# Four graph layers on one core: gathers written out with their indices read from the column table, and the last layer's plain one-hot rows compared on GpSimd

## The reference, cut to what matters

```python
x = x + L0(h)        # three rounds of normalised neighbour sums
msg = h[row] * norm[:, None]; out = segment_sum(msg, col)          # L1, then relu
x = x + L2(h)        # mean over neighbours, two 64x64 products
x = concatenate([nodes[senders], nodes[receivers], edges], axis=-1)      # L3
h = relu(x @ msg_W1 + msg_b1)
messages = relu(h @ msg_W2 + msg_b2)
agg = segment_sum(messages, receivers, num_segments=3125)
y = relu(concatenate([nodes, agg]) @ node_W1 + node_b1) @ node_W2 + node_b2
return nodes + layernorm(y)
```

## Time and profile before

| | |
|---|---|
| median of 3 runs | 1106.03 us (1105.96 to 1106.82) |
| span of the profiled execution | 1325.8 us |
| mean granted TensorE clock | 0.862 |
| POOL busy | 592.2 us (45%), of it 503.5 us in the 514 gathers |
| DVE busy | 830.9 us (63%) |
| ACT busy | 452.6 us (34%) |
| PE busy | 1006.6 us (76%) |

### The profile page before, as it was taken

The page is one execution under the profiler, slowest core; times in us unless marked ns, Lnnn a source line. Parts: engine busy times, 40 slices in busy tenths (PEclk is TensorE's granted clock), DMA queues, the critical chain, the costliest instruction groups (busy, mean ns, idle before and its releaser), DMA issues.

```text
span 1325.8 us, 24512 instructions
## 1 busy us (share of the span) xinstructions
PE 1006.6 (76%) x6145; PEld 618.1 (47%) x6145; DVE 830.9 (63%) x2605; ACT 452.6 (34%) x1035; POOL 592.2 (45%) x763
## 2 busy tenths in 40 slices
PE   3788887996667767667696787777787878777685
PEld 2566553553444545445355444434444534444443
DVE  8988877357645556757657554565555555555556
ACT  3677771011434333334013232232232323222232
POOL 6533330000665666654003656555555555555550
PEclk9677778998887788877797899999888998999997
DMA  2000006001111111100523533333333333333331
GB/s 54 2 0 0 0 0 243 1 1 22 24 23 19 20 21 22 21 19 17 168 63 75 138 81 79 76 76 76 77 73 77 75 71 77 75 73 78 72 75 34
DMA packets 145110, 72.80 MB, mean 55 GB/s; under 512 B 111917, under 2 KB 136698, under 8 KB 144922
## 3 DMA queue, kind: packets, MB, share of 16 engines
q1 hardware_dynamic: 127224, 54.98, 16.0%
q0 software_dynamic: 16448, 16.88, 6.9%
q10 hardware_dynamic: 1378, 0.22, 0.1%
HBM read 59.66 MB, written 12.35 MB: 54 GB/s over the span
## 4 chain that ended last, share of the span: by engine, by line
PE 41%; another core or an unknown queue 20%; issue 16%; DVE 12%; ACT 6%; DVEq 2%; POOL 1%; ACTq 1%; DMA 1%; SPq 1%; POOLq 0%
PE seg L1628 10%; PE big L1658 5%; PE big L1552 4%; PE seg L1683 4%; PE seg L1755 3%; PE big L1791 3%; PE seg L1802 2%; ACT A L1345 2%; PE seg L1566 2%; PE big L1781 1%; ACT A L1466 1%; PE seg L1696 1%; ACT A L1472 1%; PE seg L1823 1%
## 5 line engine op out<-in xcount | busy, mean ns | idle before, releaser
L1221 POOL DMA_INDIRECT A<-table,idx x338 | 327.3, 968 | 260.6 <-ACT idx L1317 154.2
L1221 POOL DMA_INDIRECT pair<-table,idx x176 | 176.2, 1001 | 126.8 <-ACT idx L1317 65.0
L1755 PE MATMUL seg<-A 128*128 128x384 f16 (+1 forms) x624 | 137.6, 370 | 44.5 <-issue 19.1
L1466 ACT COPY A<-big 128x512 f32<-128x512 f32 x104 | 61.1, 587 | 249.7 <-remote 156.7
L1345 ACT CAST A<-big 128x500 f32 x208 | 125.4, 603 | 48.0 <-PE big L1557 25.9
L1791 PE MATMUL big<-A 128*128 128x512 f32 x208 | 114.1, 631 | 33.6 <-ACT A L1466 28.3
L2033 DVE COPY A<-seg 128x512 f32<-128x512 f32 x52 | 36.0, 691 | 162.3 <-remote 150.6
L1683 PE MATMUL seg<-A,cur 128*64 128x160 f32 x750 | 94.8, 353 | 46.0 <-issue 45.9
L1397 ACT COPY A<-big 128x500 f32<-128x500 f32 x120 | 66.5, 576 | 181.4 <-remote 113.8
L1755 PEld LDWEIGHTS seg<-A 128*128 128x128 f16 x624 | 60.3, 106 | 140.5 <-issue 91.0
L1658 PE MATMUL big<-A 128*128 128x300 bf16 x480 | 106.1, 367 | 18.8 <-issue 10.4
(11 more groups left out here) (307 smaller groups left out, 1809.6 us busy)
## 6 DMA issues: line engine op xcount, KB each, us to landing
A<-in_edge_attr_dram SPq DMA_DIRECT2D x103, 128.0 KB
A<-drel_flat SPq DMA_DIRECT2D x104, 126.0 KB
spilled_adjacency<-A SPq DMA_DIRECT2D x1, 7074.0 KB, 21.8
A<-spilled_adjacency SPq DMA_DIRECT2D x6, 1152.0 KB, 11.8
A<-table,idx POOLq DMA_INDIRECT x338
A<-pr_table SPq DMA_DIRECT2D x104, 31.5 KB
pair<-table,idx POOLq DMA_INDIRECT x176
A<-low_flat SPq DMA_DIRECT2D x78, 32.0 KB
```

The source lines that it names most:

```text
L1221: pool.indirect_dma_start(out=row(q, j), out_offset=None, in_=table, in_offset=bass.IndirectOffsetOnAxis(ap=idx[:, q, j:j + 1], axis=0)).t ...
L1466: nc.scalar.copy(x_t[:, r, :], big[:, r, :]).then_inc(x_t_ready[r], 1)
L1755: op = nc.tensor.matmul(made[:, 0:held.shape[2] * D], hot_low[:, u, m, :], held[:, k, :, :], start=(m == 0 and k == 0), stop=(m == 3 and k ...
```

## The change: what it does

1. POOL's two gather loops are written out: 176 and 338 gathers stand one after the other in its stream, and each reads its index column straight from `src_i`. The tile `idx`, its semaphores and ACT's 148 copies are gone. In layer 1 a gather waits for `seg_done[q]` alone, in the last layer for `transposed` alone.
2. The last layer's plain one-hot rows are made on POOL, one instruction of 128 x 42 for each tile (416 in all), one behind each gather slot, six groups behind the gathers (HOTS_LAG). The first of a group waits for `seg_done` of its pair of groups. DVE's 52 instructions of 128 x 336 are gone.
3. PE's `window_sums` waits for the one-hot rows of both groups.

```diff
-            def gathers(g, row, slot_free):
-                pool.wait_ge(table_stored, 32 * (g + 1))
-                with pool.Fori(0, (IT1, IT)[g]) as it:
-                    for q in range(Q):
-                        pool.wait_ge(idx_ready[q], g * IT1 + it + 1)
-                        slot_free(it, q)
...
+            def gather_tile(row, tile, landed):
+                pool.indirect_dma_start(
+                    out=row, out_offset=None, in_=table,
+                    in_offset=bass.IndirectOffsetOnAxis(ap=src_i[:, tile:tile + 1], axis=0)).then_inc(landed, 16)
+            def gathers1():
+                pool.wait_ge(table_stored, 32)
+                pool.wait_ge(ev("src_kept"), 1)
+                for it in range(IT1):
                     for q in range(Q):
+                        pool.wait_ge(seg_done[q], 1 + it)
                         for j in range(G):
+                            gather_tile(row1(q, j), it * (Q * G) + q * G + j, gathered[q])
+            def gathers3():
+                pool.wait_ge(table_stored, 64)
+                for q in range(Q):
+                    pool.wait_ge(seg_done[q], 1 + IT1)
+                for g in range(GROUPS + HOTS_LAG):
+                    it, q = g // Q, g % Q
+                    if g < GROUPS:
+                        pool.wait_ge(transposed[q % 2], 1 + 2 * it + q // 2)
+                    for j in range(G):
+                        if g < GROUPS and not (q in MADE and j == 2):
+                            gather_tile(X[:, q, j, 0:D], it * (Q * G) + q * G + j, gathered[q])
+                        if g >= HOTS_LAG:
+                            tile_hots(g - HOTS_LAG, j)
+            def tile_hots(g, j):
+                it, q = g // Q, g % Q
+                if j == 0:
+                    pool.wait_ge(seg_done[q | 1], it + (1 + IT1))
+                op = pool.tensor_scalar(onehot3[:, q, j, :], iota_r[:, 0:GW], drel[:, g * G + j:g * G + j + 1], None, ALU.is_equal)
+                if j == G - 1:
+                    op.then_inc(onehot_ready[q], 1)
...
-            steps(act, [(0, next_idx), (2, node_relu), (3, copy_rows), (4, hidden), (5, message_relu)])
+            steps(act, [(2, node_relu), (3, copy_rows), (4, hidden), (5, message_relu)])
...
                 pe.wait_ge(msg_ready[1], k + 2)
+                pe.wait_ge(onehot_ready[q - 1], it + (IT1 + 1))
                 pe.wait_ge(onehot_ready[q], it + (IT1 + 1))
...
-            steps(dve, [(1, receivers), (5, message), (0, senders), (4, plain_hots), (0, node_norm),
+            steps(dve, [(1, receivers), (5, message), (0, senders), (0, node_norm),
```

More of the change, by code:

```diff
@@ L60 @@
 NODES_LAG = 5
+HOTS_LAG = 6
 OUTS = (slice(0, T // (G * Q) - NODES_LAG), slice(T // (G * Q) - NODES_LAG, NC))
@@ L834, in dense_path @@
         rdeg = sb("rdeg", [P, NC])
-        idx = sb("idx", [P, Q, G], I32)
         dst_c = pair[:, 0:TK]
@@ L981, in dense_path @@
         gathered = [sem(f"gathered{q}") for q in range(Q)]
-        idx_ready = [sem(f"idx_ready{q}") for q in range(Q)]
         onehot_ready = [sem(f"onehot_ready{q}") for q in range(Q)]
@@ L998, in dense_path @@
         table_ready, table_stored = sem("table_ready"), sem("table_stored")
-        gathers_begun = sem("gathers_begun")
         tail_loaded = sem("tail_loaded")
@@ L1214, in gathers @@
                     for q in range(Q):
-                        pool.wait_ge(idx_ready[q], g * IT1 + it + 1)
-                        slot_free(it, q)
-                        pool.sem_inc(gathers_begun, 1)
+                        pool.wait_ge(seg_done[q], 1 + it)
                         for j in range(G):
[L1219 to L1229, removed]
+                            gather_tile(row1(q, j), it * (Q * G) + q * G + j, gathered[q])
[12 more added lines that the diff above has]
+                            tile_hots(g - HOTS_LAG, j)
@@ L1276, in on_gpsimd @@
             pool.memset(acc_mem[D:2 * D, 0:NPAD], 0.0).then_inc(ev("lower_cleared"), 1)
-            gathers(0, row1, rows_summed)
+            gathers1()
             def clear_sums(k):
@@ L1290, in on_gpsimd @@
                 clear_sums(k)
-            gathers(1, lambda q, j: X[:, q, j, 0:D], rows_transposed)
+            gathers3()
         def steps(eng, stages, between=lambda s: None):
@@ L1314, in nodes_done @@
             return q == at and not (isinstance(it, int) and it < NODES_LAG)
-        def copy_idx(it, q):
-            nc.scalar.copy(idx[:, q, :], src_i[:, bass.ds(it * (Q * G) + q * G, G)]).then_inc(idx_ready[q], 1)
         def on_scalar(act):
@@ L1377, in on_scalar @@
                 copy_sums(n)
-            act.wait_ge(ev("src_kept"), 1)
-            for q in range(Q):
-                copy_idx(0, q)
             for k in range(ROUNDS):
@@ L1386, in on_scalar @@
                 nc.scalar.copy(acc_t[:, 4 * k * P:4 * k * P + n], seg[0:D, k % 2, 0:n]).then_inc(ev("conv1_t"), 1)
-            def next_idx1(it, q):
-                act.wait_ge(seg_done[q], 1 + it)
-                copy_idx(it, q)
             def keep_block(b, buf, more):
@@ L1409, in rows_behind @@
             def rows_behind(b, q):
-                summed = SUM_AT.get(b * Q + q - 1)
-                if summed is not None and summed + Q < Q * IT1:
-                    next_idx1(summed // Q + 1, summed % Q)
                 to_sum = SUM_AT.get(b * Q + q + 1)
@@ L1418, in on_scalar @@
                 keep_block(b, b % 2, rows_behind)
-            for q in range(Q):
-                act.wait_ge(seg_done[q], 1 + IT1)
-                copy_idx(0, q)
             copy_sums(3)
@@ L1454, in on_scalar @@
             act.wait_ge(ld_l3, 13 * 16)
[L1456 to L1460, removed]
             def copy_rows(it, q):
@@ L1879, in plain_hots1 @@
                                   drel[:, t:t + G].rearrange("p (j a) -> p j a", a=1).broadcast_to([P, G, GW]),
[L1880 to L1888, removed]
                                   ALU.is_equal).then_inc(onehot_ready[q], 1)
```

## The result

The changed kernel takes 1257.41 us (median of 4 runs, 1257.2 to 1262.54), the kernel before beside it 1106.42 (4 runs). The ratio is 1.137, 95% interval 1.135 to 1.139: 151 us slower. The forecast was 1164 us, 58 us slower, with a range of 1085 to 1225 us; the time lies above the range.

What follows compares the result with a forecast made beforehand. POOL, at 1.25 us a gather, was taken to bound both gather stages. Comparisons on POOL 62, less 4 for index copies and 0 for DVE's relief, gave +58 us on 1106: 1164 us, range 1085 to 1225.

Steps and rivals of the forecast that it cites:

- What bounds the kernel: Both gather stages: POOL at 1.25 us a gather bounds, about 447 us for the last layer, PE right behind.
- Index copies: ACT's 148 copies and POOL's waits for them go, both gather stages: 0 to 20 us gained, 4 taken.
- DVE's comparisons: Last layer: 25.8 us leave DVE, worth 0 to 10 us, taken as 0 while POOL bounds.
- The new waits: POOL's wait for `seg_done` and PE's second wait in `window_sums`: some tenths of a us or 0, latency hidden.
- POOL's comparisons: Last layer: 416 instructions of 128 x 42 on POOL, 0 to 0.60 us each, taken as 0.15, 62 us.
- Rival C: VectorE and GpSimd shut each other out in the last layer, 0.35 us a comparison: 1248 us; chance 0.10.
- Rival A: POOL's comparison fits into the 0.30 us pause behind each gather, only small gains remain: 1098 us; chance 0.27.
- Rival B: POOL's timed gather is shorter than in the profile, say 1.05 us, so POOL has slack: 1089 us; chance 0.16.

Runs made afterwards that it cites:

- undisturbed profile: Profile of the kernel before with POOL's two gather loops written out and ACT's index copies kept: 1106.61 us, ratio 0.9999, span 1107.2 us.
- written-out gathers: Kernel before with gathers written out, reading index columns directly, ACT's copies gone, comparisons left on DVE: 1103.33 us, ratio 0.9968; repeated 1102.53 us, ratio 0.9967.

## Why the prediction was wrong, point by point

*What bounds the kernel: right.* The stalls in the profile of before were taken for that execution's own and POOL's floor for real. The undisturbed profile of the same kernel has L3 at 428 us, where the step had 422 of gathers, and PE right behind it. A reading that had spent the profile's slack would have come out at no change. That the two floors are some 10 us apart is measured by the run with one gather less.

*Index copies: right in size.* 4 us were taken, 3.3 to 4.4 us measured (1106.61 less 1103.33 beside it, and 1106.88 of before less 1102.53 in the later pair). What became late next is `transposed`, as said. The place is off: the gain was to lie in layer 1, where POOL's waits for ACT turn out to be 0.6 us in the undisturbed profile, and of what was gained 1.3 to 2.6 us lie in the last layer. So there is some luck in the 4.

*DVE's comparisons: right.* 0 taken, 0 measured (1102.27 against 1102.53).

*The new waits: small, as said.* They were taken as 0; together with 416 fills they cost 7 us.

*POOL's comparisons: this step failed.* It took 0.15 us net each, 62 us. The measured price is (581.6 - 427.0) / 416 = 0.37 us, 155 us (L3 of the change from 649.2 to 1230.8, of the written-out gathers from 647.4 to 1074.4, the last start of each gather line and the gather's length). Two sizes in it were off. The length was worked out as 0.1 us fixed and 4.1 ns a column, 0.27; it is 0.30 and 2.6 ns, 0.41. One row gives one equation, and the fixed part was guessed. The row was also far from the case (one partition, f32 input), and the measured split gives only 0.30 + 208 x 0.0026 = 0.84 for its 0.96. The products of 6 columns with 0.236 us each already spoke against a fixed part of 0.1. And the overlap was counted too high: 0.12 us was taken off the length, the runs show 0.04. The pause does take in some 0.09 us (0.30 became 0.04 + 0.17), but the gather behind the comparison is 0.08 us longer. Two comparisons in a row take 0.83 us in the stretch shown, 0.77 by the median of the 74 such pairs. Saving and loss nearly cancel, so that the net price is near the whole length.

The bound of 0.60 us a comparison held the truth, the range did not: it stopped at 0.30 us. Rival C has the right size by luck (1248 us). Its mechanism is VectorE in the way, and a comparison with VectorE idle beside it takes 0.410 us against 0.413 for all; what VectorE adds is some 7 of the 155 us. The prediction set the Trainium skill's rule on the shared port pair (SBUF — State Buffer) beside this rival and expected from it a cost above 0.15 us and some loss of time for VectorE. Both came, but the first in the main for another reason. The trace agrees with the rule in part, in the longest comparisons and fills and in L1964 (343 ns against 277); no run isolates it. Rival A is false for a comparison and true for a fill: something of 0.15 us does vanish in the pause. Rival B is false: the gather keeps 1.25 us in profiles whose span agrees with the timed runs.

## What to carry to other kernels

An engine at its floor pays for nearly every instruction added to it, however small its share of a span reads (here only the fill that fits into the pause was free); find the floor as count times start-to-start spacing, and hold it against the timed run, not against a profile that ran 20% longer. Price a small instruction on GpSimd by its fixed part, from a row of the same kind and of like size, and if there is none, from two rows of different size; work that must go there should go in few wide instructions (here 31 us for 52, 154 for 416). Before moving work off an engine, ask what leaving it out would win: here nothing.

## What the runs showed of the hardware that was not expected

- An indirect gather of 128 rows of 256 bytes keeps GpSimd for 1.25 us, 0.945 and a pause of 0.30, in a stalled profile, a free one, from a loop or written out. A fill of 0.15 us in the pause is free (1.26 us).
- A comparison (TENSOR_SCALAR) on GpSimd takes 0.306 us for 1 column and 0.413 for 42, a two-input subtraction (TENSOR_TENSOR) 0.77 us for 336. The recorded length is not the price: against a constant it reads 0.32 us, and the kernel is 10 us slower.
- Behind a comparison a gather is 0.08 us longer (1.03 us), whether VectorE is idle or not; behind a fill or the two-input instruction it is 0.95 and 0.96. Why is not shown.
- PE's granted clock in the last layer is 0.97 in the kernel before with its loop written out, and 0.87 in the changed kernel, where PE waits for POOL; its busy time reads 407 and 470 us for nearly the same instructions (2231 and 2219).
